# An expert's weights fetched two transfers per item over four items, instead of four double-size transfers at its predecessor's first item

## The chip, the cores and the metric

The kernel runs on one core of a Trainium2 chip. The metric is the device time of one execution in microseconds (us), and the number to predict is the median time of the changed kernel.

## The reference, cut to what matters

An attention block comes first, then a mixture of experts with 8 experts, of which each token uses 2. There are 8192 tokens of 512 features.

```
logits  = rms_normed(x) @ router_logits                # 8 experts
choices = top 2 experts of each token
for each expert e, over the rows of x that chose it:
    gate, up = row @ w_gate[e]                         # 512 -> 2 x 512
    y        = (gelu(gate) * up) @ linear[e]           # 512 -> 512
out = x + gb * sum over the 2 choices of weight * y    # weight: softmax of the logits, renormalized
```

Everything is float32. The kernel gets that precision by splitting each operand into a high and a low part and adding three products of them.

## The kernel before

There are three phases. The first computes queries, keys and values, and beside it splits the experts' weights into high and low parts, which it stores in DRAM (`expert_split`). The second finishes the attention, routes each token, and scatters the rows of each expert into a list in DRAM (`expert_rows`). The third, to which most of the change belongs, runs the experts.

Phase 3 walks over 135 items. An item is 128 rows of one expert. A table in SBUF gives each item's first row, its expert (`tables[.,1,i]`) and its number within that expert (`tables[.,2,i]`, called `of_e`). The given inputs route the tokens so that the eight experts have 34, 21, 9, 17, 3, 17, 5 and 23 items, and the last 6 items are empty (counted from the reference's own choices).

The engines run the items as a software pipeline, each with its order written out by hand:

- TensorE, item i: `gate(i)` (12 matmuls, after `x_lo` of i and after the expert's weights), `up(i)` (12), `down(i-1)` (12, after `act_lo` of i-1). Then item i+1.
- ScalarE, item i: issue its half of the loads `arow<-act_rows` of i-1 (after the store `act_rows<-hact` of i-1 has landed), then `next_weights(i-1)`, then `gelu(i)` (after gate(i)), `act_hi(i-1)`, `x_hi(i+1)`, `gb_rows(i-1)`.
- VectorE, item i: `turn_x(i+1)`, `turn_act(i-1)` twice, `act_lo(i-1)` twice, `glu(i)` (writes `hact`, after gelu(i) and up(i)), `x_lo(i+1)`, `out_rows(i-1)`.
- SyncE: the store of `hact` as soon as it is there, its half of the loads `arow`, then the rows `xrow` and `meta` of three items ahead.
- GpSimd: the accumulating scatter `out_rows<-orow`.

So the activations of an item make a round trip through DRAM: `hact` is stored, loaded back turned in blocks, transposed, split, and only then used by `down`. Between hact of an item and its down lies about one item of matmuls.

The weights of an expert are 6 MB (high and low parts). `wbuf` has two halves, so that one expert computes while the next is loaded. `next_weights` runs on ScalarE's queue in every item: it reads the item's expert and `of_e` into registers, and for an expert's first item it waits until that expert's own weights are there and until the half is free, and issues four transfers of 1.5 MB for the next expert. The weights of expert 0 are loaded by SyncE at the end of phase 2, and those of expert 1 by ScalarE before the first gelu of phase 3. Short experts matter for this: the fifth has three items.

Of the kernel before, what the change touches and what calls it, by code (L numbers as in the profile page):

```python
# [28 lines left out]
F32 = mybir.dt.float32  # L29
# [8 lines left out]
P = 128  # L38
B, S, C = 2, 4096, 512
E, H = 8, 512  # L40
# [12 lines left out]
EW = FC * 2 * H + (H // P) * C  # L53
DOWN = FC * 2 * H
QW = 1536
QPE = EW // QW
KQW = 2 * FC * C // 4
UNIT = 512
PER_PIECE = QW // UNIT
# [9 lines left out]
EARLY = 3  # L69
# [6 lines left out]
def at_least(eng, sem, value):  # L76

    if isinstance(value, int) and value <= 0:
        return
    eng.wait_ge(sem, value)  # L80
# [27 lines left out]

def build(nc, x, c_t, wmod, wqkv, wproj, b_proj, r_w, r_scale, pes, moe_w, out):
    qd = nc.dram_tensor("q_rows", (NG * P, FC * GT), F32, kind="Internal").ap()  # L110
    wd = nc.dram_tensor("expert_split", (E * QPE * P, 2 * QW), F32, kind="Internal").ap()
    mod_d = nc.dram_tensor("mod_rows", (B, 4 * C), F32, kind="Internal").ap()
    xs = nc.dram_tensor("expert_rows", (E * CAP + P, ROW), F32, kind="Internal").ap()
    ad = nc.dram_tensor("act_rows", (P, H), F32, kind="Internal").ap()
# [3 lines left out]
    def sb(stack, name, shape, dt, side=None):  # L118
        return stack.enter_context(nc.sbuf_tensor(name, shape, dt, side=side) if side else nc.sbuf_tensor(name, shape, dt))

    def sem(name):
        return keep.enter_context(nc.semaphore(name))
# [26 lines left out]
    tables = sb(keep, "tables", [P, 3, ITEMS], I32)  # L149
# [14 lines left out]
    sp_hl = [sb(ph1, f"split_{k}", [P, QW], F32R) for k in ("hi", "lo")]  # L164
# [86 lines left out]
    wbuf = sb(ph3, "wbuf", [P, 2 * 2 * EW], F32R)  # L251

    def f32(ap):

        return ap.bitcast(F32)
# [14 lines left out]
    s_qst, s_wst, s_zst = sem("q_stored"), sem("split_stored"), sem("zero_stored")  # L270
# [34 lines left out]
    s_w, s_xt, s_xthi, s_xtlo = sem("weights_loaded"), sem("x_turned"), sem("x_hi_ready"), sem("x_lo_ready")  # L305
# [3 lines left out]
    s_o, s_cur, s_gb0, s_gbr, s_or, s_add = sem("down_done"), sem("cur_ready"), sem("gb0_ready"), sem("gb_rows_step"), sem("out_rows_ready"), sem("rows_added")  # L309
# [5 lines left out]
    def wait_apart(eng, sem, value):  # L315


        at_least(eng, sem, value)
        if not isinstance(value, int):
            eng.sem_inc(s_passed, 1)  # L320
# [59 lines left out]

    assert GPB == 8

    def load_piece(eng, e, half, q):

        eng.dma_start(f32(wbuf[:, bass.ds(half * 2 * EW + q * 2 * QW, 2 * QW)]),  # L385
                      wd[bass.ds((e * QPE + q) * P, P), :]).then_inc(s_w, 16)

    def act_rows_back(eng, i, half):

# [6 lines left out]
    def phase1_over(eng):  # L396
# [4 lines left out]
        eng.wait_ge(s_qst, 16 * NG)  # L401
        eng.wait_ge(s_wst, 32 * E * QPE)
        eng.wait_ge(s_gab, B)

    def phase2_over(eng):

        for t in range(TPG):
            eng.wait_ge(s_scat[t], SCAT * NG)
        eng.wait_ge(s_pad0, 16)
        eng.wait_ge(s_x1st, 16 * NG)  # L410
        eng.wait_ge(s_zst, 32)
        eng.wait_ge(s_it, ITEM_STEPS)
# [7 lines left out]
    def _(sp):  # L420
# [10 lines left out]
        for f in range(FC):  # L431
            at_least(sp, s_lo, f - 1)
            sp.dma_start(raw[:, f % 2, 0:KQW], wqkv[:, f * KQW:(f + 1) * KQW]).then_inc(s_raw[f % 2], 16)

# [24 lines left out]
        def store_expert(g, s):  # L459
            sp.wait_ge(s_elo, 2 * g + s + 1)  # L460
            for k in range(2):
                sp.dma_start(wd[bass.ds((2 * g + s) * P, P), k * QW:(k + 1) * QW], f32(sp_hl[k][:, :])).then_inc(s_wst, 16)

        for s in range(2):
            load_expert_raw(0, s, 0)
# [66 lines left out]
        def early_weights():  # L532

            sp.wait_ge(s_on, HG * NG)
            for q in range(EARLY):
                sp.wait_ge(s_x1, TPG * (NG - 1) + q)
                load_piece(sp, 0, 0, q)

        run_groups2(sp, group2, before_last=early_weights)


        for q in range(EARLY, QPE):
            load_piece(sp, 0, 0, q)
        phase2_over(sp)

        def load_rows(i, at):
# [226 lines left out]
    def _(act):  # L773
# [5 lines left out]
        def split_hi(loads, half, dst, width=QW):  # L779
            act.wait_ge(s_raw[half], 16 * loads)  # L780
            act.activation(dst, raw[:, half, 0:width], ACT.Copy).then_inc(s_hi, 1)
# [25 lines left out]
        def kq_hi(f):  # L807
            split_hi(f // 2 + 1, f % 2, wq[0][:, f * KQW:(f + 1) * KQW], KQW)

# [192 lines left out]
        def x_hi(i, at):  # L1002
            act.wait_ge(s_xt, i + 1)
            at_least(act, s_u, i)
            act.activation(x_t[0][:, :], XT_B[at % 2][:, :], ACT.Copy).then_inc(s_xthi, 1)  # L1005

        def gelu(i):
            act.wait_ge(s_g, i + 1)
            at_least(act, s_h, i)
            act.activation(gact[:, :], G_B[:, :], ACT.Gelu_apprx_tanh).then_inc(s_ga, 1)  # L1010
# [13 lines left out]
        def next_weights(i):  # L1024

            e = act.value_load(tables[0:1, 1, bass.ds(i, 1)], min_val=0, max_val=E - 1)  # L1026
            of_e = act.value_load(tables[0:1, 2, bass.ds(i, 1)], min_val=0, max_val=ITEMS)  # L1027
            with act.If(e > 0):
                with act.If(e < E - 1):
                    with act.If(of_e < 1):  # L1030
                        wait_apart(act, s_w, 16 * QPE * (e + 1))
                        wait_apart(act, s_o, i)
                        nxt = act.value_load(tables[0:1, 1, bass.ds(i, 1)], min_val=0, max_val=E - 2) + 1
                        for q in range(QPE):
                            load_piece(act, nxt, nxt & 1, q)

        x_hi(0, 0)
        act.wait_ge(s_w, 16 * QPE)
        for q in range(QPE):
            load_piece(act, 1, 1, q)  # L1040
        gelu(0)
        x_hi(1, 1)

# [16 lines left out]
    def _(dve):  # L1060
# [74 lines left out]
        def kq_lo(f):  # L1135
            dve.wait_ge(s_hi, f + 1)
            dve.wait_ge(s_raw[f % 2], 16 * (f // 2 + 1))
            cols = slice(f * KQW, (f + 1) * KQW)
            tt(wq[1][:, cols], raw[:, f % 2, 0:KQW], f32(wq[0][:, cols]), ALU.subtract).then_inc(s_lo, 1)

# [593 lines left out]
    def _(pe):  # L1734
# [32 lines left out]
        def product(dst, parts, n, stationary, moving):  # L1767

            k = 0
            for f in range(n):  # L1770
                for a, b in PASSES[:parts]:
                    last = mm(dst, stationary(a, f), moving(b, f), start=(k == 0), stop=(k == parts * n - 1))  # L1772
                    k += 1
            return last
# [228 lines left out]
        half = TPG // 2  # L2003
# [12 lines left out]
        def expert_of(i):  # L2016
            return pe.value_load(tables[0:1, 1, bass.ds(i, 1)], min_val=0, max_val=E - 1)

        def weights(e, at):

            base = pe.snap((e & 1) * (2 * EW), min_val=0, max_val=2 * EW)
            return lambda k, f: wbuf[:, bass.ds(base + (at(f) // QW * 2 * QW + k * QW + at(f) % QW), 512)]

        def gate(i, e):
            pe.wait_ge(s_xtlo, i + 1)
            pe.wait_ge(s_w, 16 * QPE * (e + 1))
            at_least(pe, s_ga, i)
            product(G_B[:, :], 3, FC, lambda a, f: x_t[a][:, f * P:(f + 1) * P], weights(e, lambda f: f * H)).then_inc(s_g, 1)

# [14 lines left out]

        e = expert_of(0)
        gate(0, e)
        up(0, e)

# [51 lines left out]
```

## Time and profile before

| what | value |
|---|---|
| time, median of 3 runs | 2404.31 us (2396.66 to 2406.8) |
| time of the profiled execution | 2396.8 us |
| its span | 2395.0 us |
| mean granted TensorE clock | 0.956 of full |
| busy TensorE, VectorE, ScalarE, GpSimd | 91%, 62%, 33%, 37% of the span |
| phase 3 | about 1124 us to the end |

The span is what the profile covers, from the first instruction to the last. The execution's own time is 1.8 us longer. In the rows further down, "PE" is TensorE's matmuls, "DVE" VectorE, "ACT" ScalarE, "SP" SyncE, "POOL" GpSimd. A name with q (ACTq) is the engine's sequencer, which issues transfers and handles registers. A bracket at the end of a row gives the engine's idle time before it and what ended it.

### The profile page before, as it was taken

Reading aid. Unit: us, or ns where it says so; the run is one execution under the profiler, and the core shown is the slowest. Engines: PE = TensorE matmul, PEld = TensorE weight load, DVE = VectorE, ACT = ScalarE, POOL = GpSimd, SP = SyncE. Lnnn points to the kernel's source line nnn. Section 1 sums busy time; section 2 is a strip of 40 time slices with the busy share of each in tenths; the row PEclk is TensorE's granted clock in tenths of the full one; section 3 lists DMA queues with packets and bytes.
Section 4 is the critical chain, followed back from the end, with each engine's and each line's share of the span. In section 5 each row is a group of like instructions: output and inputs, shape, how many; then the busy total and the mean of one; then the engine's idle time right before and its main releaser. Section 6 shows DMA issues by size and latency. Waiting matters only on the chain.

```text
span 2395.0 us, 44013 instructions
## 1 busy us (share of the span) xinstructions
PE 2177.2 (91%) x9280; PEld 1644.1 (69%) x9281; DVE 1478.8 (62%) x3611; ACT 785.6 (33%) x1531; POOL 894.1 (37%) x684
## 2 busy tenths in 40 slices
PE   7999999999889888893899997997989789989997
PEld 5688878888555554552678886876768668768786
DVE  6555555554689888883566664664556446646665
ACT  4244444443344333431223332332223223223332
POOL 5476655665366666674111111111111111111111
PEclk9999999999999999996999998999999889999999
DMA  7666645555335544457555556556655666665554
GB/s 236 226 203 209 207 154 189 201 181 198 141 142 210 187 183 183 182 197 289 130 122 125 123 125 195 125 124 199 167 155 124 201 192 125 163 158 123 128 123 93
DMA packets 289443, 403.60 MB, mean 169 GB/s; under 512 B 49998, under 2 KB 188238, under 8 KB 280654
## 3 DMA queue, kind: packets, MB, share of 16 engines
q1 hardware_dynamic: 215808, 266.64, 35.5%
q0 software_dynamic: 30640, 74.29, 15.2%
q10 hardware_dynamic: 42912, 61.75, 7.1%
q8 instruction: 29, 0.48, 0.1%
q14 instruction: 54, 0.44, 0.1%
HBM read 210.57 MB, written 191.98 MB: 168 GB/s over the span
## 4 chain that ended last, share of the span: by engine, by line
PE 43%; DMA 6%; ACTq 1%; issue 1%; DVE 1%; POOL 0%; ACT 0%; SPq 0%; DVEq 0%
PE bank L1772 29%; PE bank L2041 15%; DMA act_rows<-hact 3%; DMA arow<-act_rows 2%; DMA meta<-expert_rows 1%; ACTq L385 1%; DVE hact L1672 0%; ACTq L393 0%; ACT act_t_hi L1017 0%; POOL expert_rows L750 0%; DVE act_t_lo L1684 0%; DVE bank L1678 0%; DMA expert_rows<-padrow,pad_to 0%; ACTq L1026 0%; ACTq L1027 0%
## 5 line engine op out<-in xcount | busy, mean ns | idle before, releaser
L1772 PE MATMUL bank<-wbuf,x_t_hi 128*128 x2160 | 685.2, 398 | 40.1 <-DVE x_t_lo L1666 39.7
L764 POOL DMA_INDIRECT out_rows<-orow,cur_tok x135 | 209.0, 1548 | 1058.2 <-DVE orow L1704 954.3
L1772 PEld LDWEIGHTS bank<-wbuf,x_t_hi 128*128 128x128 f32 x2160 | 408.1, 189 | 143.0 <-issue 44.2
L2041 PE MATMUL bank<-wbuf,act_t_hi 128*128 x1080 | 357.0, 413 | 81.4 <-DVE act_t_lo L1684 81.2
L1772 PE MATMUL bank<-wbuf,x_t_lo 128*128 x1080 | 429.0, 397 | 0.0
L2041 PEld LDWEIGHTS bank<-wbuf,act_t_hi 128*128 128x128 f32 x1080 | 211.6, 197 | 139.2 <-issue 88.2
L1772 PEld LDWEIGHTS bank<-wbuf,x_t_lo 128*128 128x128 f32 x1080 | 204.4, 189 | 49.8
L1010 ACT ACTIVATE gact<-bank 128x512 f32<-128x512 f32 x135 | 80.8, 598 | 466.3 <-PE bank L1772 356.3
L2041 PE MATMUL bank<-wbuf,act_t_lo 128*128 x540 | 221.6, 410 | 0.0
L1678 DVE STREAM_TRANSPOSE bank<-arow 128x256 f32<-128x256 f32 x270 | 106.0, 438 | 164.1 <-DMA arow<-act_rows 164.1
L727 POOL DMA_INDIRECT expert_rows<-rows,dest x128 | 134.7, 1053 | 115.0 <-issue 63.5
L1701 DVE SCALAR_TENSOR_TENSOR gbr<-modbc,in_b,gb 128x512 f32<-128x512 f32 x135 | 101.5, 752 | 116.2 <-ACT gb L1022 116.2
L1672 DVE TENSOR_TENSOR hact<-bank,gact 128x512 f32<-128x512 f32 x135 | 93.2, 691 | 127.9 <-PE bank L1772 127.8
L1022 ACT ACTIVATE gb<-modbc,in_b 128x512 f32<-128x512 f32 x135 | 97.7, 724 | 201.9 <-DVE in_b L1698 201.9
L1108 DVE TENSOR_SCALAR hf<-bank,modcol 128x128 f32<-128x128 f32 x256 | 87.2, 403 | 95.5 <-PE bank L1752 95.3
L1005 ACT ACTIVATE x_t_hi<-bank 128x512 fp32r<-128x512 f32 x135 | 80.9, 600 | 198.1 <-PE bank L1772 179.0
L629 POOL TENSOR_TENSOR k_lo<-k_f,k_hi 128x512 fp32r<-128x512 f32 x64 | 88.9, 1390 | 123.4 <-ACT k_hi L816 123.1
L1684 DVE TENSOR_TENSOR act_t_lo<-bank,act_t_hi 128x256 fp32r<-128x256 f32 x270 | 102.1, 420 | 46.0 <-ACT act_t_hi L1017 31.4
L2041 PEld LDWEIGHTS bank<-wbuf,act_t_lo 128*128 128x128 f32 x540 | 106.4, 197 | 26.3
L625 POOL TENSOR_TENSOR z_lo<-xg,z_hi 128x512 fp32r<-128x512 f32 x64 | 83.3, 1303 | 98.5 <-ACT z_hi L805 98.5
L1660 DVE STREAM_TRANSPOSE bank<-xrow 128x512 f32<-128x512 f32 x135 | 96.9, 718 | 37.2 <-DMA meta<-expert_rows 37.2
L1704 DVE SCALAR_TENSOR_TENSOR orow<-bank,cur_w,gbr 128x512 f32<-128x512 f32 x135 | 101.4, 751 | 24.9 <-PE bank L2041 20.1
(226 smaller groups left out, 4138.9 us busy)
## 6 DMA issues: line engine op xcount, KB each, us to landing
wbuf<-expert_split ACTq DMA_DIRECT2D x28, 1536.0 KB, 12.8
xrow<-expert_rows SPq DMA_DIRECT2D x540, 64.0 KB, 1.9
act_rows<-hact SPq DMA_DIRECT2D x135, 256.0 KB, 2.0
expert_split<-split_hi SPq DMA_DIRECT2D x32, 768.0 KB, 3.5
expert_split<-split_lo SPq DMA_DIRECT2D x32, 768.0 KB, 5.8
arow<-act_rows SPq DMA_DIRECT2D x270, 64.0 KB
arow<-act_rows ACTq DMA_DIRECT2D x270, 64.0 KB
xg<-in_x SPq DMA_DIRECT2D x16, 1024.0 KB, 5.3
```

Of the source, the lines that this page charges most:

```text
L629: pool.tensor_tensor(k_hl[t % 2][1][:, :], k_f[t % 2][:, :], f32(k_hl[t % 2][0][:, :]), ALU.subtract).then_inc(s_klo, 1)
L727: pool.indirect_dma_start(out=xs, out_offset=bass.IndirectOffsetOnAxis(dest[par][:, k, t:t + 1], 0), in_=rows[par][:, t, :], in_offset=Non ...
L764: pool.indirect_dma_start(out=out, out_offset=bass.IndirectOffsetOnAxis(cur_tok[at % 2][:, 0:1], 0), in_=orow[at % 2][:, :], in_offset=Non ...
L1022: act.activation(gb0[:, :], modbc[:, 0, 3, :], ACT.Copy, scale=in_b0[:, 0:1]).then_inc(s_gb0, 1)
L1660: dve.transpose(XT_B[at % 2][:, :].rearrange("c (f a i) -> c a f i", f=FC, a=NBLK), xrow[at][:, :].rearrange("i (a f c) -> i a f c", a=NBL ...
L1672: tt(hact[:, :], U_B[:, :], gact[:, :], ALU.mult).then_inc(s_h, 1)
L1678: dve.transpose(HT_B[h][:, 0:2 * P].rearrange("c (f a i) -> c a f i", f=2, a=NBLK), arow[:, :].rearrange("i (a f c) -> i a f c", a=NBLK, f ...
L1684: tt(act_t[1][:, cols], HT_B[h][:, 0:2 * P], f32(act_t[0][:, cols]), ALU.subtract).then_inc(s_htlo, 1)
L1701: gbs.did(stt(gbr[:, :], modbc[:, 1, 3, :], in_b1[:, 0:1], gb0[:, :], ALU.mult, ALU.add))
L1704: stt(orow[at % 2][:, :], O_B[:, :], cur_w[:, 0:1], gbr[:, :], ALU.mult, ALU.mult).then_inc(s_or, 1)
L1772: last = mm(dst, stationary(a, f), moving(b, f), start=(k == 0), stop=(k == parts * n - 1))
L2041: last = mm(O_B[:, :], act_t[a][:, f * P:(f + 1) * P], moving(b, f), start=(f == 0 and (a, b) == PASSES[0]), stop=(f == H // P - 1 and (a, ...
```

## The change

The transfers of an expert's weights become half as big (768 KB), and there are eight. Two of them are issued with each of the first four items of the expert before. If that expert has fewer than four items, the rest is issued with its last one; whether an item is the last is seen by comparing its expert with the next item's, which is read into a register in every item (`e_after`). Expert 1 is handled like the others, so the four transfers ahead of the first gelu are gone. The layout of `expert_split` in DRAM is changed so that each transfer's rows lie together, and the two places that wait for an expert's weights count 16 x 8 instead of 16 x 4.

```diff
+LOADS = 2 * QPE
+PACE = 2
...
-    def load_piece(eng, e, half, q):
-        eng.dma_start(f32(wbuf[:, bass.ds(half * 2 * EW + q * 2 * QW, 2 * QW)]),
-                      wd[bass.ds((e * QPE + q) * P, P), :]).then_inc(s_w, 16)
+    def load_weights(eng, e, half, n):
+        eng.dma_start(f32(wbuf[:, bass.ds(half * 2 * EW + n * QW, QW)]),
+                      wd[bass.ds((e * LOADS + n) * P, P), :]).then_inc(s_w, 16)
...
-                sp.dma_start(wd[bass.ds((2 * g + s) * P, P), k * QW:(k + 1) * QW], f32(sp_hl[k][:, :])).then_inc(s_wst, 16)
+                sp.dma_start(wd[bass.ds((2 * (2 * g + s) + k) * P, P), :], f32(sp_hl[k][:, :])).then_inc(s_wst, 16)
...
-                load_piece(sp, 0, 0, q)
+                for k in range(2):
+                    load_weights(sp, 0, 0, 2 * q + k)
...
         def next_weights(i):
             e = act.value_load(tables[0:1, 1, bass.ds(i, 1)], min_val=0, max_val=E - 1)
+            e_after = act.value_load(tables[0:1, 1, bass.ds(i + 1, 1)], min_val=0, max_val=E - 1)
             of_e = act.value_load(tables[0:1, 2, bass.ds(i, 1)], min_val=0, max_val=ITEMS)
-            with act.If(e > 0):
-                with act.If(e < E - 1):
-                    with act.If(of_e < 1):
-                        wait_apart(act, s_w, 16 * QPE * (e + 1))
-                        wait_apart(act, s_o, i)
-                        nxt = act.value_load(tables[0:1, 1, bass.ds(i, 1)], min_val=0, max_val=E - 2) + 1
-                        for q in range(QPE):
-                            load_piece(act, nxt, nxt & 1, q)
+            def share(later):
+                nxt = act.value_load(tables[0:1, 1, bass.ds(i, 1)], min_val=0, max_val=E - 2) + 1
+                nth = act.value_load(tables[0:1, 2, bass.ds(i, 1)], min_val=0, max_val=LOADS // PACE - 1 - later) + later
+                for k in range(PACE):
+                    load_weights(act, nxt, nxt & 1, nth * PACE + k)
+            with act.If(e < E - 1):
+                with act.If(of_e < LOADS // PACE):
+                    wait_apart(act, s_w, 16 * LOADS * (e + 1))
+                    wait_apart(act, s_o, i)
+                    share(0)
+                    with act.If(e_after > e):
+                        for later in range(1, LOADS // PACE):
+                            with act.If(of_e < LOADS // PACE - later):
+                                share(later)
...
-        act.wait_ge(s_w, 16 * QPE)
-        for q in range(QPE):
-            load_piece(act, 1, 1, q)
```

## Rows read from the trace of the kernel before

**Rows 1.** The page's costliest groups: the matmuls of `down`.
```profile
L2041 PE MATMUL bank<-wbuf,act_t_hi 128*128 x1080 | 357.0, 413 | 81.4 <-DVE act_t_lo L1684 81.2
```
**Rows 2.** Waits of PE in phase 3: us in total, times, longest.
```profile
PE bank L2041 <- DVE act_t_lo L1684: 81.2, 14, 11.3
PE bank L1772 <- DVE x_t_lo L1666: 39.7, 2, 26.4
```
**Rows 3.** Windows in phase 3: us, then busy time of each engine, clock, DMA, GB/s.
```profile
1165.00:1430.00 265.00, 264.10 (x1125) 211.25 (x1125) 168.40 (x405) 80.92 (x156) 48.60 (x32) 1.00 0.58 125
1430.00:1480.00 50.00, 36.68 (x144) 28.60 (x143) 21.18 (x52) 9.62 (x20) 5.76 (x5) 0.86 0.69 210
```
**Rows 4.** The chain that ended last: gate and up, where items begin (start, us).
```profile
1426.78 5.64 PE bank L1772 x24
...
1477.22 5.62 PE bank L1772 x24
...
1621.10 5.64 PE bank L1772 x24
...
1661.64 5.62 PE bank L1772 x24
```
**Rows 5.** Timeline of PE at the first such place: down after each gap.
```profile
1442.86 0.72 PE L2041 MATMUL bank<-wbuf,act_t_hi 128*128 x2 [2.03 <-DVE act_t_lo L1684]
...
1462.97 1.22 PE L2041 MATMUL bank<-wbuf,act_t_hi 128*128 x2 [11.29 <-DVE act_t_lo L1684]
```
**Rows 6.** Timeline of ACT there: gelu of a plain item, then of a loading item.
```profile
1429.63 0.60 ACT L1010 ACTIVATE gact<-bank 128x512 f32<-128x512 f32 x1 [2.76 <-PE bank L1772]
...
1435.42 0.84 ACTq L393 DMA_DIRECT2D arow<-act_rows  x2
1438.88 2.29 ACTq L385 DMA_DIRECT2D wbuf<-expert_split  x4
1441.29 0.60 ACT L1010 ACTIVATE gact<-bank 128x512 f32<-128x512 f32 x1 [5.98 <-issue]
```
**Rows 7.** The chain, narrowed to 1436 to 1469 us: ScalarE's sequencer, step by step.
```profile
1436.30 0.05 ACTq L1026
...
1436.91 0.05 ACTq L1027
...
1437.52 0.04 ACTq L1028
...
1437.95 0.28 ACTq L1033
...
1438.49 0.04 ACTq L385
...
1438.88 0.41 ACTq L385
...
1439.55 0.38 ACTq L385
...
1442.86 0.69 DVE hact L1672
```
**Rows 8.** Timeline of SP's transfers: round trip of a plain, then a loading item.
```profile
1433.33 0.35 SPq L560 DMA_DIRECT2D act_rows<-hact  x1
1435.42 0.81 SPq L393 DMA_DIRECT2D arow<-act_rows  x2
...
1443.64 0.35 SPq L560 DMA_DIRECT2D act_rows<-hact  x1
1452.91 0.81 SPq L393 DMA_DIRECT2D arow<-act_rows  x2
```
**Rows 9.** Line L385 from 1438 to 1446 us: the four 1.5 MB transfers.
```profile
DMA to landing us min/median/max: 7.4/13.1/19.5
```
**Rows 10.** The window after a gap of 2.27 us (columns as in rows 3).
```profile
1888.90:1892.30 3.40, 3.40 (x10) 2.63 (x9) 1.25 (x6) 0.72 (x1) 0.00 (x0) 0.50 1.06 364
```
**Rows 11.** Timeline of ACT: first transfer for the sixth and the seventh expert.
```profile
1883.53 0.40 ACTq L385 DMA_DIRECT2D wbuf<-expert_split  x1
...
1925.53 0.39 ACTq L385 DMA_DIRECT2D wbuf<-expert_split  x1
```
**Rows 12.** The start of phase 3: PE's wait ahead of gate(1).
```profile
1145.02 1.21 PE L1772 MATMUL bank<-wbuf,x_t_hi 128*128 x2 [13.28 <-DVE x_t_lo L1666]
```
**Rows 13.** The chain at that place, whole phase: what gate(1) waited for.
```profile
1127.78 14.68 DMA meta<-expert_rows
```
**Rows 14.** The same line's issues over the whole run: KB each, us to landing.
```profile
meta<-expert_rows SPq DMA_DIRECT2D x135, 6.0 KB, 3.6
```

More of the change, by code:

```diff
@@ L110, in build @@
     qd = nc.dram_tensor("q_rows", (NG * P, FC * GT), F32, kind="Internal").ap()
-    wd = nc.dram_tensor("expert_split", (E * QPE * P, 2 * QW), F32, kind="Internal").ap()
+    wd = nc.dram_tensor("expert_split", (E * LOADS * P, QW), F32, kind="Internal").ap()
     mod_d = nc.dram_tensor("mod_rows", (B, 4 * C), F32, kind="Internal").ap()
@@ L536, in early_weights @@
                 sp.wait_ge(s_x1, TPG * (NG - 1) + q)
-                load_piece(sp, 0, 0, q)
+                for k in range(2):
+                    load_weights(sp, 0, 0, 2 * q + k)
         run_groups2(sp, group2, before_last=early_weights)
-        for q in range(EARLY, QPE):
-            load_piece(sp, 0, 0, q)
+        for n in range(2 * EARLY, LOADS):
+            load_weights(sp, 0, 0, n)
         phase2_over(sp)
@@ L2025, in gate @@
             pe.wait_ge(s_xtlo, i + 1)
-            pe.wait_ge(s_w, 16 * QPE * (e + 1))
+            pe.wait_ge(s_w, 16 * LOADS * (e + 1))
             at_least(pe, s_ga, i)
```

## Prediction

> **What bounds the kernel now.** I began with the page's costliest groups: the only idle time of TensorE in phase 3 that amounts to anything is in front of `down` [rows 1]. TensorE's own list of waits says the same: 14 waits for `act_t_lo`, 81.2 us, and two for `x_t_lo` [rows 2]. The windows then show that this idle time isn't spread. From 1165 to 1430 us TensorE is busy 264.1 of 265 us at full clock with 125 GB/s moving, and from 1430 to 1480 us, where expert 2's weights are fetched, it is busy 36.7 of 50 us at a mean clock of 0.86 with 210 GB/s [rows 3]. So phase 3 is bound by TensorE, but for one disturbance per expert and one at its start.
>
> The timelines split a disturbance in two. A plain item takes 8.43 us (gate and up 5.62, down 2.81).
> - The first gap, 2.03 us [rows 5], comes from ScalarE's queue. In a plain item gelu starts as soon as gate is done (1429.63) and would start 8.43 later, at 1438.06. In the loading item it starts at 1441.29 and had been kept by "issue" [rows 6], 3.23 us late. The gap is 1.2 us less, so that much lateness is free.
> - The second gap, 11.29 us [rows 5], comes from the transfers. The store of `hact` lands 2.09 us after its issue in a plain item (1433.33 to 1435.42), and 9.27 us after it behind the weights (1443.64 to 1452.91) [rows 8]; the loads back are late as well.
> - The clock falls after a gap. After the small one it was sometimes at its lower level, 1.2 GHz, for 3.4 us (0.50 in [rows 10], after a gap of 2.27 us).
>
> Between item starts 1426.78 and 1477.22 lie four items, 50.44 us for 33.73: 16.7 lost. Between 1621.10 and 1661.64 lie three: 15.2 lost [rows 4]. There are six such places, so 6 x 16.0 = 96 us.
>
> **What the change removes.** The six bursts: 96 us. And the burst for expert 1 at the start: gate(1) waits 13.28 us [rows 12] for row loads of which the last took 14.68 us [rows 13] where its kind takes 3.6 in the median [rows 14]. That frees 14.68 - 3.6 = 11 us. Together 107 us.
>
> **What it adds, ScalarE.** I take the loading item's steps from the narrowed chain [rows 7], from the issue of the `arow` loads, A = 1435.42, which end 0.84 later [rows 6]. A register load from the table costs 0.61 us (L1026 to L1027, L1027 to L1028). There are now three ahead of the branches: +0.61. Branches and waits until L1033 cost 0.43; one branch goes at the front and one comes at the end. The load at L1033 is 0.54, and there are two: +0.54. From L385's first register step to the first transfer is 0.39, which the longer address may lengthen by 0.1. A transfer is 0.67 with its registers (1438.88 to 1439.55), and two fewer are issued: -1.3. Sum: 0.61 + 0.54 + 0.1 - 1.3 = 0.0. So a paced item keeps ScalarE as long as a loading item did: gelu at A + 5.85 (1441.29 - 1435.42 = 5.87), the first transfer at A + 3.46 + 1.15 = A + 4.6. Only there are 27 paced items (four for six experts, three for the fifth) where there were six.
>
> What is queued behind it on ScalarE is gelu, then act_hi. `hact` waits for gelu, and down for act_lo. hact starts 1.57 after gelu (1442.86), its store is issued 0.78 later [rows 8], and lands 2.09 after that if nothing is in the way. Only then can the next `arow` loads be issued. So in consecutive paced items there is a loop that doesn't contain TensorE at all: 5.85 + 1.57 + 0.78 + 2.09 + d = 10.3 + d us, where d is what the weights add to the store. TensorE needs 8.43.
>
> **What it adds, the store's delay d.** The pair is 1.5 MB issued from A + 4.6. The same bytes in the burst landed 7.4 us after issue at the earliest, so at A + 12.0 [rows 9]. The store is issued at A + 8.2 and would land at A + 10.3. They overlap at the end. From above: the store lands with the last of the weights and then its own share of time, d = 2.4 (in the burst, with far more ahead of it, d was 7.2). From below: d = 0, if the weights are through by then or the store gets its turns. Nothing excludes either. I take the middle, 1.2: the pair has 1.7 us left when the store should have landed, and the store needn't wait for all of it. The Trainium skill (DMA: Bandwidth & Descriptors, Queues, rings and completion order) says that each DMA engine goes round its queues packet by packet. The trace agrees in that the store took 9.27 us while the four transfers' last landed at 19.5.
>
> **Sum for an expert of four items or more.** Item 1: the gap of about 2.1 (2.03 here) and 0.15 of restart = 2.3. Its successor starts behind in the loop, so items 2 to 4 take 11.5 each, 3.05 more than 8.43: 9.1. Then 1.0 for the clock: while the loop bounds, a slow clock costs nothing, but after the last paced gap 3.4 us at half rate cost up to 1.7. Sum 12.4. Five experts (of 34, 21, 9, 17 and 17 items): 62. The seventh has 5 items, and its last pair, issued in the fifth item, is needed one item later: it lands at A + 12.0, about 13.1 after that item's start, and gate wants it at 11.5: 12.4 + 1.7 = 14.
>
> **The expert of three items.** The starts of the loads for its successor and the one after lie 42.0 us apart [rows 11], which is 3 x 8.43 + 16.7. Now its third share and the rest, four transfers, are issued while gate of the next expert is already wanted. They land at A + 4.6 + 7.4 + 4.0 (the four of a burst landed 7.4 to 19.5, so 4.0 for each 1.5 MB) = A + 16.0, about 17 us after the item's start. With 3 us for the clock, as behind the long gap of today (16.7 lost [rows 4], less 2.0 and 11.3 of idle [rows 5]), that is 20. The two items before add 2.3 and 3.05. Sum 25.5.
>
> **At no cost.** The third register load in the 108 other items: ScalarE's registers end at A + 2.1 today, gelu of a plain item is at A + 2.6 (1427.0 to 1429.63 by the period), so gelu slips by 0.1 and 1.2 are free; without that cover 0.1 each would be 11 us. The store layout of phase 1 and the doubled issues for expert 0: SyncE idles there, and the bytes are the same. The empty items load nothing.
>
> **Total.** Removed 107, added 62 + 14 + 25.5 = 101.5: a gain of 5.5 to 7 us, say 6.5. On the profiled execution 2396.8 becomes 2390; that execution is 7.5 us under the median of the runs, 2404.3. Against the median: 2398.
>
> **Rivals.**
> - *The store isn't delayed* (d = 0). Items 2 to 4 cost 1.85 each: 8.8 per expert, 44 + 10.5 + 23 = 77.5. Gain 30, 2374. For it: only the end of the pair overlaps the store. Against: the weights have 3.6 us of head start on the store, and [rows 9] has no transfer that lands under 7.4. The Trainium skill's fit (DMA: Bandwidth & Descriptors, Anatomy of one DMA, given for GpSimd's path: 2.0 us plus bytes over 436 GB/s) would land the pair an estimated 5.6 us after its issue, at the time at which the store should land, and so speaks for this rival; no transfer of 1.5 MB in [rows 9] landed that soon.
> - *The loop is longer* (slower, the other side): d = 2.4, so items 2 to 4 cost 4.2 and the fifth 1.0. 17 per expert, 85 + 19 + 28 = 132. Loss 25, 2429. It decides from d = 1.6 on, where the gain is gone. For it: d = 2.4 is what follows if the pair lands as the burst's first transfer did. Against: half-size packets give the store its turn twice as often.
> - *The gaps vanish*, ScalarE's time being hidden. Only the three-item expert costs: gain 85, 2319. Against it: the loading item's 5.87 us gave a gap of 2.03 [rows 5, 6], and by the sum above a paced item's sequencer time is the same.
> - *It doesn't pace*: excluded, the first four items of each expert meet the condition.
>
> **How the numbers follow.** Forecast case 0.45 (d from 0.7 to 1.7), undelayed store 0.27, longer loop 0.22, vanishing gaps 0.06. Half a per cent, 12 us, is what a measurement tells from nothing. The forecast case reaches from a gain of 17 to a loss of 4, and about a tenth of it, 0.05, is above 12. Faster 0.27 + 0.06 + 0.05 = 0.38; slower 0.22, of which some 0.01 stays within; same the rest, 0.40. The range reaches to both rivals, 2374 to 2425; the forecast case's own is 2387 to 2409.
>
> **What would show it.** In the profile after: 27 gaps in front of `down`, not 12, 2 us for each first one and 3 for the next; gelu released by "issue" 5.8 us after the `arow` loads; stores landing in about 3.3 us in paced items; one gap of 15 us or more in front of gate in the expert after the three-item one; gate(1) some 11 us earlier. It is wrong if ScalarE's steps are shorter or longer than by [rows 7] (0.3 us each is 7 us in all), or if d isn't near 1.2 (0.1 is about 2 us).

## The result: slower by 4%, and the profile after

| | before | after |
|---|---|---|
| median of the runs, us | 2403.72 (2396.66 to 2406.8, 4 runs) | 2505.05 (2498.66 to 2505.91, 4 runs) |
| after over before | | 1.042 (95%: 1.0391 to 1.0449) |
| profiled execution, us | 2396.8 | 2504.71 |
| its span, us | 2395.0 | 2502.9 |

The forecast was 2398 with a range to 2425. The change costs 101 us. The matmuls of `down`, the first of the page's groups that was read before [rows 1], now wait 51 us longer. The page's queue of instruction loads, which the prediction doesn't mention, has four times its packets. The page of the kernel after (groups: busy, mean ns, idle before; queues: packets, MB, share of 16 engines):
```profile
L2050 PE MATMUL bank<-wbuf,act_t_hi 128*128 x1080 | 377.1, 433 | 132.8 <-DVE act_t_lo L1693 132.8
...
q14 instruction: 213, 1.74, 0.2%
```
The same queue's row in the kernel before:
```profile
q14 instruction: 54, 0.44, 0.1%
```
PE's waits in phase 3 after, which answer to [rows 2]: us in total, times, longest.
```profile
PE bank L2050 <- DVE act_t_lo L1693: 132.8, 54, 5.7
PE bank L1781 <- DVE x_t_lo L1675: 27.1, 2, 25.2
PE bank L1781 <- DMA wbuf<-expert_split: 23.6, 8, 17.9
```
No wait for `act_t_lo` is as long as the 11.3 us of before, but there are 54 where there were 14, and 27 were forecast. 28 of them lie in the loading items as they are defined below, 26 (47.9 us) in plain ones. The window over plain items shows it; before, TensorE was busy 264.1 of 265 us [rows 3]:
```profile
1200.00:1430.00 230.00, 218.06 (x907) 170.30 (x906) 134.04 (x330) 61.47 (x126) 38.67 (x25) 0.99 0.54 117
```
12 of 230 us are idle at nearly full clock, with fewer bytes moving than before.

To place the loss I took the start of each item's gelu from ScalarE's timeline (135 per run) and summed what each step from one gelu to the next has above the plain item's 8.435 us. 39 steps belong to the items in which a kernel here loads weights, or to those right behind ("loading items" below: the first six of each expert with a successor, three of the short one), 95 to the rest ("plain items"). Only the last kernel, eighths, loads in two items more.

| us above 8.435 per item | 39 loading items | 95 plain items |
|---|---|---|
| before | 109.8 | 2.0 |
| after | 161.0 | 61.5 |

Together 110.7 more, where the spans differ by 107.9. So there are two losses: the loading items got dearer by 51 us instead of cheaper, and the plain items, which the forecast had "at no cost", lost 60.

**The plain items.** From gelu to gelu they take 7.85, 8.95, 8.21 and 10.9 us, over and over: 35.9 for four, where before there were 33.7. Four is the number of items that the loop of `run_items` (L373) writes out in one round. ScalarE's timeline at the end of a round, after:
```profile
1361.69 0.60 ACT L1013 ACTIVATE gact<-bank 128x512 f32<-128x512 f32 x1 [3.29 <-DVE bank L1687]
...
1369.89 0.60 ACT L1013 ACTIVATE gact<-bank 128x512 f32<-128x512 f32 x1 [3.07 <-PE bank L1781]
...
1377.37 0.88 ACTq L395 DMA_DIRECT2D arow<-act_rows  x2
1380.78 0.60 ACT L1013 ACTIVATE gact<-bank 128x512 f32<-128x512 f32 x1 [5.52 <-issue]
```
and the chain that ended last, narrowed to the same place (start, us, what):
```profile
1374.54 0.04 ACT gb L1025
1374.58 0.03 issue
1374.61 0.04 ACTq L373
1374.66 2.38 issue
1377.04 0.06 ACTq L373
```
At the loop's branch back ScalarE's sequencer stands still for 2.38 us, for nothing that the profile shows on any semaphore. The packets of the instruction queue fall into the same rounds, five of 8 KB (1.74 MB over 213) in each.

**The loading items.** SP's and ScalarE's timelines of a paced item after, which answer to [rows 6] and [rows 8]. SP:
```profile
1470.93 0.81 SPq L395 DMA_DIRECT2D arow<-act_rows  x2
1472.73 1.87 SPq L555 DMA_DIRECT2D xrow<-expert_rows  x4
1474.79 0.35 SPq L557 DMA_DIRECT2D meta<-expert_rows  x1
1480.47 0.35 SPq L563 DMA_DIRECT2D act_rows<-hact  x1
1484.96 0.81 SPq L395 DMA_DIRECT2D arow<-act_rows  x2
```
ScalarE:
```profile
1470.93 0.85 ACTq L395 DMA_DIRECT2D arow<-act_rows  x2
1476.45 1.14 ACTq L387 DMA_DIRECT2D wbuf<-expert_split  x2
1478.12 0.60 ACT L1013 ACTIVATE gact<-bank 128x512 f32<-128x512 f32 x1 [10.42 <-issue]
```
The loop of the forecast is there, from `arow` loads to `arow` loads without TensorE: 1470.93 to 1484.96, 14.0 us, where 11.5 were forecast. Medians over 26 of the 27 paced items (A is the issue of the item's `arow` loads; the last item of the three-item expert, whose store comes long after its transfers, is left out here and in all such medians below): first transfer at A + 4.75 (forecast 4.6), gelu at A + 6.41 (5.85), store 4.36 us (3.3), loop 13.1.

### The profile page after: what moved, and what is told of

It is laid out like the page before. It is cut to its first block, busy times and chain, and to the rows that moved or that the text cites. A ratio compares the mean times of both kernels' runs of the same rounds, so it can differ in the third digit from the quotient of the medians.

```text
span 2502.9 us, 44793 instructions
## 1 busy us (share of the span) xinstructions
PE 2222.3 (89%) x9280; PEld 1658.0 (66%) x9281; DVE 1468.7 (59%) x3611; ACT 766.1 (31%) x1531; POOL 893.1 (36%) x684
## 3 DMA queue, kind: packets, MB, share of 16 engines
q14 instruction: 213, 1.74, 0.2%
## 4 chain that ended last, share of the span: by engine, by line
PE 15%; DMA 13%; issue 10%; ACTq 8%; DVE 6%; ACT 3%; DVEq 1%; POOLq 0%; POOL 0%; SPq 0%
PE bank L1781 9%; DMA out_rows<-orow,cur_tok 8%; PE bank L2050 5%; DMA act_rows<-hact 3%; ACTq L395 2%; ACTq L387 2%; DVE orow L1713 1%; DVE gbr L1710 1%; ACT gb L1025 1%; DMA arow<-act_rows 1%; ACTq L1031 1%; ACTq L1030 1%; ACTq L1029 1%; ACT act_t_hi L1020 1%; DVE hact L1681 1%
## 5 line engine op out<-in xcount | busy, mean ns | idle before, releaser
L2050 PE MATMUL bank<-wbuf,act_t_hi 128*128 x1080 | 377.1, 433 | 132.8 <-DVE act_t_lo L1693 132.8
L2050 PEld LDWEIGHTS bank<-wbuf,act_t_hi 128*128 128x128 f32 x1080 | 219.5, 207 | 207.2 <-issue 156.5
L2050 PE MATMUL bank<-wbuf,act_t_lo 128*128 x540 | 229.3, 425 | 0.0
L1710 DVE SCALAR_TENSOR_TENSOR gbr<-modbc,in_b,gb 128x512 f32<-128x512 f32 x135 | 101.5, 752 | 116.1 <-ACT gb L1025 116.1
L2050 PEld LDWEIGHTS bank<-wbuf,act_t_lo 128*128 128x128 f32 x540 | 112.0, 207 | 27.7
L1008 ACT ACTIVATE x_t_hi<-bank 128x512 fp32r<-128x512 f32 x135 | 81.6, 605 | 126.6 <-PE bank L1781 120.9
L1781 PE MATMUL bank<-kvp_hi,on_hi 128*128 (+1 forms) x256 | 112.7, 440 | 5.0 <-DVE on_lo L1583 3.6
```

The costliest lines, as they stand in the source:

```text
L1710: gbs.did(stt(gbr[:, :], modbc[:, 1, 3, :], in_b1[:, 0:1], gb0[:, :], ALU.mult, ALU.add))
L2050: last = mm(O_B[:, :], act_t[a][:, f * P:(f + 1) * P], moving(b, f), start=(f == 0 and (a, b) == PASSES[0]), stop=(f == H // P - 1 and (a, ...
```

## The experiments

Each ratio is against runs of the kernel before on the same chip; their medians were 2416.65 for the first four kernels, 2416.24 for the next four and 2399.17 for the last three, so ratios are compared, not times.

### 1. Code that never runs

The kernel before with four copies of a load of two pieces under a condition that can't hold there. The branch around them lies inside the first item's, so plain items execute nothing new. The loop's code grows from 172 to 384 instructions in the compiled listing of ScalarE's loop body (waits not counted). After the change it has 369.
```diff
                         for q in range(QPE):
                             load_piece(act, nxt, nxt & 1, q)
+                        with act.If(of_e > 1):
+                            for _ in range(DEAD):
+                                nxt = act.value_load(tables[0:1, 1, bass.ds(i, 1)], min_val=0, max_val=E - 2) + 1
+                                nth = act.value_load(tables[0:1, 2, bass.ds(i, 1)], min_val=0, max_val=2) + 1
+                                for q in range(2):
+                                    act.dma_start(f32(wbuf[:, bass.ds((nxt & 1) * 2 * EW + nth * 2 * QW, 2 * QW)]),
+                                                  wd[bass.ds((nxt * QPE + nth) * P, P), :]).then_inc(s_w, 16)
```


> The kernel before, with code added to next_weights that is never executed: inside the branch of an expert's first item, under a condition that is false there, four blocks like the change's share (two register loads and two transfers each). The body of ScalarE's item loop becomes about as long as the changed kernel's (384 instructions against 369, where before has 172); the instructions that run are the same but for one branch in six items. Theory A (the longer loop no longer stays in the sequencer's memory and its code is fetched anew in each round): queue 14 carries some 213 packets instead of 54, and the plain items lose about 2.2 us in four, 60 to 75 us in all. Rival B (the third register load and the paced transfers cost the time themselves): no difference from before, 2404 us. Rival C (DMA contention of the paced transfers): the same as B.

Measured: 2469.04 us, ratio 1.0223 (1.0205 to 1.0241), 52 us lost by code that isn't executed, somewhat less than the 60 to 75 expected. Its page, and ScalarE at the end of a round:
```profile
q14 instruction: 214, 1.75, 0.2%
```
```profile
1386.00 0.72 ACT L1023 ACTIVATE gb<-modbc,in_b 128x512 f32<-128x512 f32 x1 [1.47 <-DVE in_b L1706]
1388.95 0.93 ACTq L394 DMA_DIRECT2D arow<-act_rows  x2
1391.46 0.60 ACT L1011 ACTIVATE gact<-bank 128x512 f32<-128x512 f32 x1 [4.74 <-issue]
```
From the end of gb to the `arow` loads it is 2.2 us, once in four items; in the other three of the round it is 0.1 to 0.5. Plain items lose 43.9 us (2.0 before), loading items 121.6 (109.8). The length of the code alone is half of the change's loss.

### 2. The change with short code

The change, with only one catch-up share of weights written out for an expert's last item instead of three. This runs the same instructions for every expert of this input: the short expert has three items, so after its third share only one is left. The listing falls from 369 to 237.
```diff
                     with act.If(e_after > e):
-                        for later in range(1, LOADS // PACE):
+                        for later in range(1, 2):
```


> The changed kernel with the rest for short experts cut from three unrolled shares to one, which is all that this routing needs (the three-item expert has one share left); an expert of one or two items would not be served. The same instructions run; ScalarE's loop body has 237 instead of 369 instructions. Theory A: if 237 fit, queue 14 is back at some 55 packets, plain items are back at 8.43 us, and the time is 2395 to 2430 us, which is then the worth of the pacing itself (my forecast was 2398). Rivals B and C: 2505 us as in the changed kernel.

Measured: 2468.66, ratio 1.0211 (1.0191 to 1.0231), well above the 2395 to 2430 expected; the instruction queue has 55 packets again, as expected. Plain items lose 7.1 us instead of 61.5, loading items 154.1 instead of 161.0. So 54 us in the plain items and some 7 in the others were instruction loads. What remains, 2.1%, is pacing.
```profile
1476.75 0.35 SPq L563 DMA_DIRECT2D act_rows<-hact  x1
1481.83 0.81 SPq L395 DMA_DIRECT2D arow<-act_rows  x2
...
1490.77 0.35 SPq L563 DMA_DIRECT2D act_rows<-hact  x1
1494.31 0.81 SPq L395 DMA_DIRECT2D arow<-act_rows  x2
```
These are two stores on SP's timeline, of 5.08 and 3.54 us. Of its 28 gaps ahead of `down` 26 lie in the loading items, where the forecast had 27. Medians over the paced items: gelu at A + 6.43, store 4.83 (3.3 to 6.0), loop 13.7.

### 3. One register load more

```diff
             e = act.value_load(tables[0:1, 1, bass.ds(i, 1)], min_val=0, max_val=E - 1)
+            act.value_load(tables[0:1, 1, bass.ds(i + 1, 1)], min_val=0, max_val=E - 1)
```


> The kernel before with one more register load from the table in next_weights, in each item, its value unused (loop body 185 instructions against 172). Theory A: plain items unchanged, time within 2 us of before. Rival B: up to 0.6 us in each of 134 items, so up to 80 us more.

Measured: 2422.71, ratio 1.0011 (0.9995 to 1.0027): not told from nothing. A round of four plain items takes 8.28, 8.45, 8.39 and 8.64 = 33.76 us, 33.74 before: the slip of 0.1 hides in gelu's slack, as forecast. The sums have 3.5 us more in the plain items and 2.1 in the loading ones, at single places. short_rest's rounds take 33.9 to 34.2, so what plain items lose there (7.1) isn't this load alone; I haven't assigned it.

### 4. Expert 1 treated like the others

The kernel before, with the part of the change that concerns expert 1.
```diff
-            with act.If(e > 0):
-                with act.If(e < E - 1):
+            with act.If(e < E - 1):
...
         x_hi(0, 0)
-        act.wait_ge(s_w, 16 * QPE)
-        for q in range(QPE):
-            load_piece(act, 1, 1, q)
         gelu(0)
```

> The kernel before with expert 1 treated like the others only: its four transfers of 1.5 MB are issued with expert 0's first item and not ahead of the first gelu. All theories: the wait in front of gate(1) falls from 13.3 to about 2 us (11 us less), and a seventh place with the two gaps of 2 and 11 us appears in expert 0's first items (16 us more): 2404 to 2412 us.

Measured: 2422.23, ratio 1.0020 (1.0010 to 1.0031), +5.6 us. The wait of gate(1) falls from 13.28 [rows 12] to 1.87 us, and a seventh place with the burst's gaps comes in its stead: the first expert's steps sum to 17.8 above the plain ones, 13.1 before. After the change gate(1) waits 1.87 as well, so the 11 us of the forecast were freed.

### 5. Is it the size of the weights' packets?

A theory that came up here: a weights row is one packet of 6144 B in the trace, the store's are 2048 B; where the queues take turns packet by packet, the store should gain by smaller ones. So in two kernels the weights lie in blocks of 128 x 512 and move in packets of 2048 B: short_rest with that layout (short_rest_fine), and the kernel before, bursts and all (fine_burst).
```diff
-        eng.dma_start(f32(wbuf[:, bass.ds(half * 2 * EW + n * QW, QW)]),
-                      wd[bass.ds((e * LOADS + n) * P, P), :]).then_inc(s_w, 16)
+        eng.dma_start(f32(wbuf[:, bass.ds(half * 2 * EW + n * QW, QW)]).rearrange("p (u n) -> p u n", n=UNIT),
+                      wd[bass.ds((e * LOADS + n) * PER_PIECE * P, PER_PIECE * P), :].rearrange("(u p) n -> p u n", p=P)).then_inc(s_w, 16)
```


> The kernel short_rest (the change with a loop body that stays in memory) with one thing more: the weights are laid out in DRAM in blocks of 512 columns, so that its transfers consist of packets of 2 KB instead of 6 KB. Theory D (in a paced item the store of hact waits its turn behind packets of the weights, one for each of its own, so its delay goes with the size of those packets): the store lands in 2.7 to 3.5 us in paced items instead of 3.5 to 5.0, items 2 to 4 of an expert take about 11.5 us instead of 13.4, and the time falls by 25 to 45 us against short_rest, to 2425 to 2445 us. Rival E (the store waits until all bytes ahead of it are through, whatever the packets): store and time as in short_rest, 2469 us.

Measured: 2467.02, ratio 1.0220 (1.0195 to 1.0245), as short_rest; the store's median is 4.51, still over 4. The theory fell for the paced items.

> The kernel before with the same layout in blocks of 512 columns, and nothing else: four transfers of 1.5 MB at each expert's first item, in packets of 2 KB instead of 12 KB. Theory D: the store behind the burst lands in about 4 us instead of 9.2. The half of the arow loads that ScalarE issues stands in the same queue as the weights, behind all of them, so most of the second gap stays: 8 to 11 us instead of 10; time 2395 to 2416 us against 2416 for before in this job. Rival E: no change of the store.

Measured: 2416.98, ratio 0.9998 (0.9984 to 1.0012). Here the packets did what they should: behind the burst the store takes 5.7 us instead of 8.9 to 9.8, and the second gap shrinks, in the step from gelu to gelu from about 5.9 us above plain to 2.2. But ScalarE now stands for some 6 us at the issue of its third and fourth transfer, until A + 11.4, and the step with the first gap grows from 3.3 to about 9 us above plain. The sum is the same. The chain at one such place (the first two issues take 0.45 and 0.42):
```profile
1459.44 2.42 ACTq L385
...
1462.14 3.77 ACTq L385
```

### 6. Fewer and earlier steps on ScalarE

The fine layout with one transfer of 1.5 MB for each item instead of two of 768 KB, with the registers used again instead of loaded twice and `e_after` read only where it is needed (paced_fine); and the same with the registers read ahead of the wait for the `arow` loads (paced_fine_early).
```diff
         def item(i, at):
+            e, of_e = item_of(i - 1)
+            if not isinstance(i, int) or i > 1:
+                gb_rows(i - 2)
             act_rows_back(act, i - 1, 1)
-            next_weights(i - 1)
+            next_weights(i - 1, e, of_e)
             gelu(i)
...
-            gb_rows(i - 1)
```


> The change rebuilt so that it costs ScalarE little: one transfer of 1.5 MB in packets of 2 KB with each of the first four items, the registers of the item reused instead of loaded again, the next item's expert loaded only in those items, the rest for short experts in three small blocks (loop body 240 instructions). Theories A and D: queue 14 at some 55 packets; gelu in paced items about 4.2 us after the arow loads instead of 6.1 to 6.8, store 2.7 to 3.3 us, so the loop has about 9.3 us an item and the gaps in front of down are under 1 us: 2340 to 2375 us, faster than before by 2 to 3%. If pacing as such costs what short_rest shows: 2450 or more.

> As paced_fine, and the two register loads of each item are done ahead of gb_rows, in ScalarE's pause before it, instead of between the arow loads and gelu. Theory: the transfer is issued about 1.2 us earlier, gelu isn't late at all in paced items, no gaps but in front of gate after the three-item expert: 2330 to 2365 us, 5 to 15 us less than paced_fine. Against it: arow loads up to 0.3 us later in all items, where about 1 us is free.

Measured: paced_fine 2436.76, ratio 1.0084 (1.0059 to 1.0108), gelu at A + 5.12, store 5.29; paced_fine_early 2425.01, ratio 1.0032 (1.0017 to 1.0047), gelu at A + 3.62, store 5.76. Both were expected to be faster than the kernel before, and neither is. ScalarE's part of the loop is cut from 6.43 to 3.62 us, and 0.93 of these 2.81 come back in a slower store (4.83 to 5.76). SP in a paced item of paced_fine_early:
```profile
1479.60 2.02 SPq L553 DMA_DIRECT2D xrow<-expert_rows  x4
1481.80 0.46 SPq L555 DMA_DIRECT2D meta<-expert_rows  x1
1483.93 0.34 SPq L561 DMA_DIRECT2D act_rows<-hact  x1
1488.63 0.81 SPq L393 DMA_DIRECT2D arow<-act_rows  x2
```
The packets of the traces show what the store ends with. In short_rest its last packet ends 0.49 to 0.65 us behind the pair's last one in 25 of the 26 items, and 0.65 us is the store's own share: 8 packets of 84 ns on each of 16 engines. The pair's last packet ends anywhere from A + 11.1 to A + 13.5, which is why the stores differ between 3.3 and 6.0. With packets of 2048 B (short_rest_fine) the distance has the same median, 0.65, and so small packets don't help. In paced_fine_early the `xrow` loads, issued by SP ahead of the store, also still have packets moving, up to about 1487; in short_rest_fine they are through before the store is issued, so they aren't the reason there.

### 7. Pacing with hardly any bytes

short_rest with 128 of the 1536 columns in each paced transfer. It leaves out eleven twelfths of the weights of experts 1 to 7, so those experts compute with the wrong weights; the number of transfers and instructions is that of short_rest. An extra load of a whole expert stands at the start.
```diff
-                    load_weights(act, nxt, nxt & 1, nth * PACE + k)
+                    load_weights(act, nxt, nxt & 1, nth * PACE + k, 128)
```


> short_rest (the change with a loop body that stays in memory), but each paced transfer carries only the first 128 of its 1536 columns; the rest of the weights of experts 1 to 7 is left out (expert 0's stand in both halves of wbuf, loaded once more at the start of phase 3, some 15 us). ScalarE runs the same instructions, the DMA engines move a twelfth of the bytes. Of an item of experts paced with two transfers, about 13 us in short_rest, this takes the part that is contention. Theory F (the loop of ScalarE and round trip with d, 10.3 + d us, is what bounds paced items, and d is some 2.5 us there): gelu 5.9 to 6.5 us after the arow loads as before, store back to 2.1 us, paced items 10.3 to 11.0 us. Rival G (ScalarE's own time isn't in the way, all comes from the transfers): paced items at 8.43 to 8.8 us. Rival H (it is ScalarE alone): unchanged, 12 to 15 us.

Measured, one execution: 2385.21. ScalarE's and SP's timelines:
```profile
1453.27 0.84 ACTq L395 DMA_DIRECT2D arow<-act_rows  x2
1458.02 1.13 ACTq L387 DMA_DIRECT2D wbuf<-expert_split  x2
1459.43 0.60 ACT L1015 ACTIVATE gact<-bank 128x512 f32<-128x512 f32 x1 [6.27 <-issue]
```
```profile
1453.27 0.81 SPq L395 DMA_DIRECT2D arow<-act_rows  x2
...
1461.77 0.35 SPq L565 DMA_DIRECT2D act_rows<-hact  x1
1463.86 0.81 SPq L395 DMA_DIRECT2D arow<-act_rows  x2
```
ScalarE's time is nearly the same (gelu at A + 6.16), the store takes 2.09 us as in a plain item, and the loop takes 10.6, as expected from the loop with d = 0. The loading items fall from 154.1 to 76.2, so the bytes are worth 2.9 us for each of 27 paced items. The windows of one loop, with all the bytes (short_rest) and without (few_bytes), columns as in [rows 3]:
```profile
1468.30:1481.80 13.50, 11.19 (x41) 8.62 (x41) 6.97 (x16) 2.36 (x5) 1.55 (x1) 0.87 0.71 195
```
```profile
1453.30:1463.90 10.60, 8.28 (x36) 6.18 (x34) 5.55 (x14) 2.36 (x5) 1.55 (x1) 1.00 0.52 112
```

### 8. Half the code that never runs

never_run with two copies, 280 instructions in the listing. It was to lie under the limit.

> never_run with half of the code that is never executed (loop body 280 instructions instead of 384; before 172, short_rest 237). Theory A says there is one length from which code is fetched anew in each round: either queue 14 stays at 54 to 56 packets and plain items at 8.43 us (the limit lies above 280), or it is well over 100 and one item in four takes over 10 us (below). I expect the first: as before.

Measured, one execution: 2448.55; 212 packets of instructions, every fourth plain item 10.5 to 10.9 us. The expectation was wrong: 259 instructions (the next kernel) are kept over a whole round, 280 aren't, and there is nothing in between: the packets are 54 to 56 or 212 to 214.

### 9. Half the bytes in each item

The change with one transfer (768 KB) in each of the first eight items, the rest of a short expert in sizes of one, two and four, registers read early: 259 instructions.
```diff
-                with act.If(of_e < LOADS // PACE):
+                with act.If(of_e < LOADS):
...
-                    share(0)
+                    nxt = nc.s_assert_within(e, 0, E - 2) + 1
+                    nth = nc.s_assert_within(of_e, 0, LOADS - 1)
+                    load_weights(act, nxt, nxt & 1, nth, 1)
...
+                        at = act.snap(nth + 1, min_val=1, max_val=LOADS)
+                        for size in (1, 2, 4):
+                            with act.If((at & size) > 0):
+                                load_weights(act, nxt, nxt & 1, nc.s_assert_within(at, size, LOADS - size), size)
```


> One transfer of 768 KB with each of the first eight items of an expert, the rest for shorter ones in three transfers of 1, 2 or 4 blocks, register loads ahead of gb_rows as in paced_fine_early (loop body 259 instructions). Theory K (the DMA engines are the limit of a paced item: a plain item keeps them busy 0.58 of 8.43 us, 1.5 MB adds 3.8 us or 0.45, together over 1, but 768 KB add only 0.23, together 0.81): items of the five long experts are at 8.43 to 9.0 us throughout; the experts of 3 and 5 items cost one gap each, about 20 and 12 us; together some 50 us lost where before has 108, so 2355 to 2375 us against 2416, 2% faster. Rival: if the store is delayed in each of the eight items by the same 2 us as in the four, the time is 2410 us or more. If the body is too long for the memory, queue 14 shows it.

Measured: 2376.69, ratio 0.9905 (0.9882 to 0.9927), faster than the kernel before by 1%; 56 packets of instructions. ScalarE and SP in a loading item:
```profile
1432.22 0.84 ACTq L395 DMA_DIRECT2D arow<-act_rows  x2
1434.23 0.40 ACTq L387 DMA_DIRECT2D wbuf<-expert_split  x1
1435.55 0.60 ACT L1013 ACTIVATE gact<-bank 128x512 f32<-128x512 f32 x1 [3.45 <-DVE bank L1692]
```
```profile
1438.55 0.35 SPq L563 DMA_DIRECT2D act_rows<-hact  x1
1441.71 0.81 SPq L395 DMA_DIRECT2D arow<-act_rows  x2
```
The store takes 3.16 us here (median 3.5) and the loop 9.5. Loading items still cost about 1 us each and up to 2, so the time is above the range expected, but `down`'s waits are nearly gone. PE's waits:
```profile
PE bank L1786 <- DMA wbuf<-expert_split: 39.2, 9, 19.7
...
PE bank L2055 <- DVE act_t_lo L1698: 24.8, 25, 5.3
```
Of what is left, a part is the price of spreading over eight items: the experts of three and of five items can't, and their weights come late (22.5 and 22.2 us above plain, the others 5 to 7 in their first six steps). The 13.0 in its plain items are mostly the seventh and eighth item of the five long experts, which load here.

The sums of all kernels, us above 8.435 per item:

| kernel | ratio | instruction packets | loading | plain |
|---|---|---|---|---|
| after | 1.042 | 213 | 161.0 | 61.5 |
| never_run | 1.0223 | 214 | 121.6 | 43.9 |
| never_run_half | one execution | 212 | 121.2 | 40.2 |
| short_rest | 1.0211 | 55 | 154.1 | 7.1 |
| short_rest_fine | 1.0220 | 56 | 159.8 | 5.7 |
| few_bytes | one execution | 55 | 76.2 | 7.0 |
| one_more_load | 1.0011 | 55 | 111.9 | 5.5 |
| expert1_alike | 1.0020 | 54 | 115.8 | 3.0 |
| fine_burst | 0.9998 | 54 | 112.7 | 1.4 |
| paced_fine | 1.0084 | 55 | 131.8 | 1.7 |
| paced_fine_early | 1.0032 | 55 | 120.9 | 2.1 |
| eighths | 0.9905 | 56 | 76.4 | 13.0 |

## Why the prediction was wrong

**What held.** The old gaps went, gate(1)'s 11 us among them. The first gap of an expert is 1.9 to 2.3 us in short_rest, 3.0 in the very first (2.1 forecast). The expert after the three-item one waits for its weights, 17.89 us; the forecast had them land 17 us after the item's start, and a gap of 15 or more. PE's timeline after:
```profile
1131.93 0.73 PE L1781 MATMUL bank<-wbuf,x_t_hi 128*128 x2 [1.87 <-DVE x_t_lo L1675]
...
1987.06 1.22 PE L1781 MATMUL bank<-wbuf,x_t_hi 128*128 x2 [17.89 <-DMA wbuf<-expert_split]
```
That expert costs 27.5 us above plain in short_rest (25.5 forecast), the one behind the five items waits 1.5 for its weights after the change (1.7 forecast). That 25.5 came so near is partly luck: the landings of the burst lie 4.7 us apart and not 4.0, since the times in [rows 9] count from issues that themselves lie 0.64 apart. The mechanism, a loop over ScalarE and the store that excludes TensorE, is right, and so is the rival on the slower side, "the loop is longer", as far as it goes.

**What failed first: "At no cost".** The forecast costed the plain items by the instructions that they execute. Nothing in it asked how long ScalarE's loop of four items had become. Shown by never_run and short_rest: code that never runs costs 52 us, and the change with short code saves 2.1%. In the change it is 54 us in plain items and some 7 in loading ones. The Trainium skill (Runtime: NRT & Kernel Launch, Instruction fetch mechanics) says that an engine holds only a small stretch of its instructions and that a taken branch out of that stretch forces a load before it can go on. The trace agrees, with 2.38 us at the loop's branch back. That page of the Trainium skill gives the store as 512 instructions for an engine like ScalarE, in two blocks of 256; the trace shows packets of 8 KB, and the boundary between 259 and 280 listed instructions. Waits aren't in that count, so these runs don't say what the size in instructions is.

**What failed second: d = 1.2, and 5.85 for ScalarE.** Both terms of the loop 5.85 + 1.57 + 0.78 + 2.09 + d were too small. Without the bytes the store takes 2.08, with them 4.83: d is 2.75, above the upper bound of 2.4. ScalarE takes 6.43 instead of 5.85 with all the bytes, 6.16 without; 0.3 of the 0.6 are longer steps of the code, 0.3 come with the bytes. For the seven experts the forecast had 62 + 14 + 25.5 = 101.5, short_rest measured 154.1: 52.6 more, of which 2.0 are the three-item expert's and 50.6 the six others'. Their steps from gelu to gelu are in the mean 3.3, three times 5.4, and 1.4 us above plain; the forecast had 2.3, three times 3.05, and 1.0. So 42 of the 50.6 lie in items 2 to 4.

**Why the bound was no bound.** Its form was right: "the store lands with the last of the weights and then its own share of time" is what the packets show in experiment 6. So the middle between the bounds, "the store needn't wait for all of it", was the wrong choice. And the bound was too small because the pair is through later than A + 12.0: its last packet ends at A + 12.6 in the median, 7.5 us after its first issue, which itself comes at A + 5.0 instead of 4.6.

What wasn't asked either is whether an item has room for the pair. A plain item uses 0.58 of the DMA engines' time [rows 3]; a pair takes some 4 us of all of them (the packets of the whole burst add up to 15.4 us on 16 engines, 3.9 for each 1.5 MB), which is 0.47 of 8.43. Together 1.05, so an item with a pair can hardly be done in 8.43 us. The windows above agree on the 4 us: in short_rest's loop the DMA engines are busy for 0.71 x 13.5 = 9.6 us, without the bytes for 0.52 x 10.6 = 5.5. But this sum isn't the cause of the loss: 1.05 alone would make 8.9 us of an item, the loop takes 13.7, and the DMA engines are busy for only 0.71 of it. Half a pair gives 0.58 + 0.24 = 0.82, and with that the kernel gets faster. eighths bears this out but doesn't single it out, since it changes ScalarE's steps as well.

**What stays open.** It stays open why the items of a round differ as they do after the change (7.85, 8.95, 8.21, 10.9): only the stop at the branch was seen, and the packets with it, not where each of the five waits. It also stays open why the pair's last packet, with which the store ends, comes 6.0 us after the first issue in one item and 8.8 in another.

## What to carry to other kernels

Count the instructions of a loop's body on each engine before you add branches to it, those that won't run too, and read the instruction queue's packets before and after: a jump there (54 to 213) is a stall at every round that no semaphore shows. Before spreading a transfer over items, add its share of the DMA engines' time to the share that an item already uses; 0.58 + 0.47 is over 1, 0.58 + 0.24 is not, though a sum under 1 isn't free either (about 1 us an item here). And when a small transfer is issued while a large one is about to end, reckon that it ends with the large one plus its own share, until a trace says otherwise: here it did in 25 of 26 items, and the middle between two bounds cost the forecast most of its error in the loading items.

## What the runs showed of the hardware that was not expected

- The instruction loads are all or nothing: up to 259 listed instructions in ScalarE's round 54 to 56 packets in the whole run, from 280 on 212 to 214. Where it was looked at, ScalarE's sequencer then stops for 2.4 us at the branch back (2.38 in the change) or starts its next loads 2.1 to 2.3 us after gb (never_run), though the executed instructions are the same.
- Of four transfers of 1.5 MB in packets of 2048 B the third and the fourth hold ScalarE's sequencer for 2.4 and 3.8 us (fine_burst), where the same bytes in packets of 12288 B take about 0.4 each (2.29 for four with their registers [rows 6]).
- The store of 128 rows behind 1.5 MB takes 4.5 us in the median with packets of 2048 B and 4.8 with packets of 6144 B, and in both its last packet ends 0.65 us (median) behind the weights' last; behind the whole burst it takes 5.7 us with packets of 2048 B instead of 9.5 with 12288 B. So packet size made a difference only behind the burst, where the store lands long before the weights are through.
